# First tiles of a mixture of experts: twelve made of five groups' rows in place of sixteen made of six groups'

## The chip, the cores and the metric

The kernel runs on one core of one Trainium2 chip. The metric is the device time of one execution in microseconds (us), the median over several runs; less is better.

## The reference

The input is 8 sequences of 1024 rows of 128 numbers (float32). Four layers follow each other, each added to its own input after a normalisation of the rows: x = x + layer(layernorm(x)).

1. A delta-rule attention with 4 heads (a short convolution, projections, a triangular solve in each chunk, a state carried from chunk to chunk, a gate, an output projection).
2. A mixture of 8 experts, top 2 of 8 for each row.
3. A linear recurrence along each sequence (three projections, two scans, a ratio, an output projection).
4. The same mixture again, with the same weights.

The mixture is the part that the change touches:

```
logits = xf @ router_w.T                                    # xf: 8192 x 128
topk_probs, topk_idx = top_k(softmax(logits), 2)            # normalised to sum 1
h   = gelu(einsum('nc,ech->neh', xf, w_fc) + b_fc)          # hidden 512
out = einsum('neh,ehc->nec', h, w_proj) + b_proj
y   = einsum('nec,ne->nc', out, combine)                    # combine: two weights a row
```

## The kernel before

The 8192 rows are held in SBUF as 8 groups (g or b, 0 to 7) of 1024 rows, and a group is 8 blocks of 128 rows. The second mixture counts its groups on, 8 to 15. Tiles are counted on in the same way, 0 to 39 and 40 to 79; where a text speaks of tile 12 of a mixture, it is the thirteenth.

**Routing.** For each group, when its rows of the layer before are ready, the kernel normalises them, finds the two experts of each row, and gives every row of every expert a place in a list in HBM (`xs`), where each expert has a region of its own. `place(g)` adds the group's counts to running counts (`run`, two buffers, even and odd groups). POOL then sends the rows: `send(g, n)` issues two indirect DMAs for each block n, so 16 for a group (L633). Their semaphore is `moe_sent0` for even groups and `moe_sent1` for odd ones.

**Tiles.** A tile is 512 rows of one expert's list (full, 31 of them) or 256 (short, 9 of them), 40 in a mixture. The first N_EARLY = 16 tiles are full ones that lie wholly in the rows of the first six groups. Their table (`early_table`: which expert, which row) is made before the last groups are routed. The table of the rest (`route_table`, five pieces) is made when all groups are counted. The constant `short_at` spreads the nine short tiles evenly from position N_EARLY to the last.

**One tile's work.** SP loads the rows (`xt`, L533) and the expert's weights (`wb`, about 1 MB, L498), each into one of four buffers. PE turns the rows (L1761), ACT and DVE split them into a high and a low part (`yTh`, `yTl`), PE multiplies with the first weights (`up`, 12 matmuls, L1773 to L1775), ACT applies the gelu and with DVE splits the result (`hidf`, `hidh`, `hidl`), PE multiplies with the second weights (`down`, 12 matmuls, L1785 to L1787), ACT adds the bias (`out_t`), PE turns the result back (L1795), DVE weighs it (`orow`, L1113), and POOL puts the rows into HBM by one indirect DMA for each block (L671).

**Order.** Each engine runs its own program in order. PE's step t is: turn(t+1), up(t), back(t-2), down(t-1). DVE's step t is: weights(t+1) (the rows' weights, which waits for the rows and the weights of tile t+1), tokens_low(t+1), hidden_low(t) with rows(t-2) in between, and then what is due in this step: choose, weigh and place of the last group in steps 2 and 3, pieces of the table from step TAIL_TABLE on. ACT has tokens_high(t+1) ahead of hidden(t). POOL's step t is: the puts of tile t, and in steps 2 to 5 (TAIL_SEND = 2) two blocks of the last group's sends, that is four DMAs. So the last group of a mixture is routed and sent beside the mixture's first tiles.

**SP's order** around the change (`moe_sync`, L506 to L536): it waits for the early table, loads two tiles' weights, waits for the sends of the first six groups (`sent`, L502), and then goes from tile to tile: rows, then weights. From tile TAIL_FILL = 9 on, in four tiles, it writes two fillers each behind the ends of the experts' lists (L485; the first waits for the counts of all groups). At tile N_EARLY - 2 it waits for the rest's table (L511), at tile N_EARLY for the fillers and for the sends of all groups. Rows and weights of tile t wait until tile t - 4 has left their buffers.

In the first mixture the attention layer's loop runs ahead, in the second the linear recurrence's loop over the groups, where the sends of group b + 5 of the mixture stand in POOL's program a group behind its routing.

Of the kernel before, what the change touches and what calls it, by code (L numbers as in the profile page):

```python
# [18 lines left out]
ALU = mybir.AluOpType  # L19
# [22 lines left out]
def bc(ap, axis, n):  # L42

    v = ap.unsqueeze(axis)
    shape = list(v.shape)
    shape[axis] = n
    return v.to_broadcast(shape)
# [33 lines left out]
def hybrid_kernel(nc, ap, out, phases=4):  # L81
    assert phases == 4
    B, L, _ = ap["hidden"].shape
    NB = B * L // P
    BPB = L // P
    E, _, HID = ap["w_fc"].shape
    HC = HID // P
    GB = 4
    GT = GB * P
# [4 lines left out]
    N_SHORT = N_HALVES - 2 * N_FULL  # L94
    assert N_SHORT >= E
    NT = N_FULL + N_SHORT
    N_EARLY = 16
    N_LATE = N_FULL - N_EARLY
    assert (2 * (B - 2) * L - E * (GT - 1)) // GT >= N_EARLY
    NST = B * L // HT  # L100
    CAP = B * L + HT
    SPARE = E * CAP
# [16 lines left out]
    with ctx:  # L119
        delta_ctx = ExitStack()  # L120

        def sb(name, shape, dt=F32):
            return ctx.enter_context(nc.sbuf_tensor(name, [P] + shape, dt))
# [19 lines left out]
        first = sb("first", [E])  # L143
# [46 lines left out]
        run = sb("run", [2, E, BPB])  # L190
# [72 lines left out]
        base = sb("base", [E])  # L263
        tab1_u = sb("tab1_u", [2, N_EARLY], U32)
        t_e = sb("t_e", [E])
# [55 lines left out]
        def s(name):  # L321
            if name not in SEMS:
                SEMS[name] = sem(name)
            return SEMS[name]
# [68 lines left out]
            return slice(C * k, C * k + C)  # L393

        N_W = 17
        TAIL_ROWS, TAIL_TURN, TAIL_LG, TAIL_RANK, TAIL_SEND, TAIL_TABLE, TAIL_FILL = 0, 1, 2, 3, 2, 5, 9
        W_LIN = 6
        LOADS = ((0, 1), (1, 2), (2, 4), (4, 6), (6, 8))

# [10 lines left out]

        short_at = {N_EARLY + round(j * (NT - 1 - N_EARLY) / (N_SHORT - 1)): j for j in range(N_SHORT)}
        assert len(short_at) == N_SHORT
# [8 lines left out]
        def blocks_of(t):  # L421

            return GB if column[t % NT] < N_FULL else HB
# [14 lines left out]
        def _(sp):  # L438
# [38 lines left out]
            def moe_sync(m):  # L477
                def sm(name):
                    return s(f"moe_{name}")

                def fill_end(e):
                    if e == 0:
                        sp.wait_ge(sm("ends"), m + 1)
                    end = sp.value_load(end_u[0:1, e:e + 1], min_val=0, max_val=SPARE - HT)
                    sp.dma_start(xs[bass.ds(end, HT), :].rearrange("(p j) c -> p j c", j=HB), bc(filler[:, :], 1, HB))\  # L485
                        .then_inc(sm("filled"), 16)

                def entry(row, t):
                    k = column[t - m * NT]
                    return tab1_u[0:1, row, k:k + 1] if k < N_EARLY else tab_u[0:1, row, k:k + 1]  # L490

                def weights(t):
                    b = t % XB
                    e = sp.value_load(entry(1, t), min_val=0, max_val=E - 1)
                    if t >= XB:
                        sp.wait_ge(sm("wts"), t - XB + 1)
                        sp.wait_ge(sm("oT"), t - XB + 1)
                    sp.dma_start(wb[:, b, :].bitcast(F32), wblob[bass.ds(e, 1)].rearrange("a p w -> p (a w)"))\  # L498
                        .then_inc(sm(f"w{b}"), 16)

                def sent(p, groups):
                    sp.wait_ge(sm(f"sent{p}"), 16 * 2 * BPB * groups)  # L502

                t0, ahead = m * NT, 2
                if m == 0:
                    sp.wait_ge(s("p_out"), 16 * N_PREP)  # L506
                    sp.wait_ge(s("p_cst"), 16)
                    sp.wait_ge(s("d_inv"), B)
                else:
                    sp.wait_ge(s("r_took"), B)  # L510
                sp.wait_ge(sm("tab1"), m + 1)  # L511
                for t in range(t0, t0 + ahead):
                    weights(t)
                for p in range(2):
                    sent(p, (m + 1) * B // 2 - 1)
                for t in range(t0, t0 + NT):
                    b, nb = t % XB, blocks_of(t)
                    if 0 <= t - t0 - TAIL_FILL < E // 2:
                        for k in range(2):
                            fill_end(2 * (t - t0 - TAIL_FILL) + k)  # L520
                    if t - t0 == N_EARLY - ahead:
                        sp.wait_ge(sm("tab"), m + 1)
                    if t - t0 == N_EARLY:
                        sp.wait_ge(sm("filled"), 16 * E * (m + 1))
                        for p in range(2):
                            sent(p, (m + 1) * B // 2)
                        if m == 0:
                            sp.wait_ge(s("spare"), 16)
                    row = sp.value_load(entry(0, t), min_val=0, max_val=SPARE)
                    if t >= XB:  # L530
                        sp.wait_ge(sm("T"), t - XB + 1)
                        sp.wait_ge(sm("wts"), t - XB + 1)
                    sp.dma_start(xt[:, b, 0:nb], xs[bass.ds(row, nb * P), :].rearrange("(p j) c -> p j c", j=nb))\  # L533
                        .then_inc(sm(f"x{b}"), 16)
                    if t >= t0 + ahead:
                        weights(t)  # L536
# [171 lines left out]
        def _(ve):  # L708
# [234 lines left out]
            def count_steps(have, base_row, what):  # L943
                ch.link(ve.tensor_tensor(n_e[:, :], have, base_row, ALU.subtract))
                ch.link(ve.tensor_tensor(over[:, :, :], bc(steps[:, :], 1, E), bc(n_e[:, :], 2, NST), what))

            def spans(cols, ks, at_e, end_e):
                n = cols.stop - cols.start
                ve.tensor_tensor(in_e[:, cols, :], bc(tiles[:, ks], 2, E), bc(at_e[:, :], 1, n), ALU.is_ge)
                return ve.tensor_tensor(in_f[:, cols, :], bc(tiles[:, ks], 2, E), bc(end_e[:, :], 1, n), ALU.is_ge)  # L950

            def rows_of_tiles(cols, ks, size, row_e):
                n = cols.stop - cols.start
                return ve.scalar_tensor_tensor(in_f[:, cols, :], bc(tiles[:, ks], 2, E), float(size), bc(row_e[:, :], 1, n),
                                               ALU.mult, ALU.add)
# [12 lines left out]
            short = slice(N_FULL, NT)  # L968

            def early_table(m):  # L970
                count_steps(run[:, 1 - B % 2, :, BPB - 1], first[:, :], ALU.is_le)
                ch.link(ve.tensor_reduce(t_e[:, :], over[:, :, 2:NST].rearrange("p e (k z) -> p e k z", z=2)[:, :, :, 0],
                                         AXX, ALU.add))
                ch.link(ve.tensor_tensor_scan(t_end[:, :], ones_row[:, 0:E], t_e[:, :], 0.0, ALU.mult, ALU.add))
                ve.tensor_scalar(took_to[:, :], t_end[:, :], float(N_EARLY), None, ALU.min)
                ch.link(ve.tensor_tensor(t_at[:, :], t_end[:, :], t_e[:, :], ALU.subtract))
                ch.link(ve.tensor_scalar(took[:, :], t_at[:, :], float(N_EARLY), None, ALU.min))
                ch.link(ve.tensor_tensor(took[:, :], took_to[:, :], took[:, :], ALU.subtract))
                ve.scalar_tensor_tensor(row0[:, :], t_at[:, :], float(-GT), first[:, :], ALU.mult, ALU.add)
                ve.scalar_tensor_tensor(base[:, :], took[:, :], float(GT), first[:, :], ALU.mult, ALU.add)  # L980
                ch.link(spans(early, early, t_at, t_end))
                tile_experts(early, N_EARLY)
                ch.link(rows_of_tiles(early, early, GT, row0))
                tile_rows(early)
                ve.tensor_copy(tab1_u[:, :, :], tab[:, :, early]).then_inc(s("moe_tab1"), 1)
# [87 lines left out]
            def moe_vector(m):  # L1073
# [42 lines left out]
                t0, t1 = m * NT, (m + 1) * NT  # L1116
                weights(t0)
                tokens_low(t0)
                for t in range(t0, t1 + 2):
                    if t + 1 < t1:  # L1120
                        weights(t + 1)
                        tokens_low(t + 1)
                    for c in range(HC):
                        if t < t1:
                            hidden_low(t, c)
                        if c == 1 and t >= t0 + 2:
                            rows(t - 2)
                    if t - t0 == TAIL_LG:
                        choose((m + 1) * B - 1)
                    if t - t0 == TAIL_RANK:  # L1130
                        weigh((m + 1) * B - 1)
                        place((m + 1) * B - 1)
                        route_ends(m)
                    if 0 <= t - t0 - TAIL_TABLE < 5:
                        route_table(m, t - t0 - TAIL_TABLE)

            moe_vector(0)

# [772 lines left out]
```

## Time and profile before

| | us |
|---|---|
| median of 3 runs | 1410.99 (1409.87 to 1417.46) |
| the profiled execution | 1409.89 |
| its span, first to last instruction | 1406.8 |
| busy: PE, DVE, ACT, POOL | 995.6, 1098.6, 717.9, 787.7 |

The first mixture lies at some 592 to 845 us of the span, the second at some 1115 to 1370. Engines: PE = TensorE matmul, PEld = TensorE weight load, DVE = VectorE, ACT = ScalarE, POOL = GpSimd, SP = SyncE, which here only issues DMAs (SPq). L12 is line 12 of the kernel. In a timeline, numbers in square brackets are the idle time of the engine ahead of the instruction and what ended it. Releasers are inferred from semaphore events; "issue" is time in which an engine waits for nothing that the profile shows.

### The profile page before, as it was taken

What the parts mean: (1) busy time and instruction counts of PE and PEld (TensorE: products, weight loads), DVE (VectorE), ACT (ScalarE), POOL (GpSimd) and SP (SyncE); (2) the same over time, 40 slices, a digit from 0 to 9 for tenths busy, and PEclk for the clock granted to TensorE, in tenths of its full rate; (3) what the DMA queues carried; (4) which work ended last, traced back from release to release, by engine and by line L of the source; (5) the groups of instructions that cost most, each with busy time, mean ns of one, the idle gap of its engine ahead of it and who ended that gap; (6) DMA issues with size and microseconds to landing.
All of it is one profiled execution on the core that took longest, in us unless ns stands there. A gap on an engine that the chain in (4) does not pass through costs nothing.

```text
span 1406.8 us, 33043 instructions
## 1 busy us (share of the span) xinstructions
PE 995.6 (71%) x11963; PEld 732.4 (52%) x11963; DVE 1098.6 (78%) x3207; ACT 717.9 (51%) x1534; POOL 787.7 (56%) x670
## 2 busy tenths in 40 slices
PE   4547768668686656399999973665554599999960
PEld 1224455545554445278888861332232478788850
DVE  1188899999999875379888864798988689788845
ACT  2444354452533212077777753765655277777740
POOL 3232256666565552627777661148777747777660
PEclk9768769586785555599999995677676699999985
DMA  5010101111111103138788843012111559788839
GB/s 136 23 45 26 47 26 58 37 47 48 58 59 38 49 28 151 51 133 286 265 280 271 293 138 120 30 49 100 39 38 37 202 181 291 246 292 279 292 103 351
DMA packets 78624, 184.32 MB, mean 131 GB/s; under 512 B 16735, under 2 KB 44826, under 8 KB 68224
## 3 DMA queue, kind: packets, MB, share of 16 engines
q1 hardware_dynamic: 51280, 142.04, 30.3%
q0 software_dynamic: 17280, 35.70, 7.3%
q10 hardware_dynamic: 9904, 4.49, 1.2%
q8 instruction: 96, 1.57, 0.5%
q14 instruction: 64, 0.52, 0.1%
HBM read 131.20 MB, written 52.79 MB: 131 GB/s over the span
## 4 chain that ended last, share of the span: by engine, by line
DVE 28%; PE 27%; POOL 18%; issue 13%; ACT 7%; DMA 6%; SPq 1%; POOLq 0%; DVEq 0%; ACTq 0%
POOL xs L633 7%; POOL res L671 6%; PE ps L1565 5%; DMA res<-orow,idt 3%; POOL rn L616 2%; DVE prod L798 2%; PE ps L1773 2%; PE ps L1774 2%; PE ps L1775 2%; DVE t_p L802 2%; PE ps L1787 2%; PE ps L1785 2%; PE ps L1786 2%; ACT ysc L1247 1%; DVE r_stats L720 1%
## 5 line engine op out<-in xcount | busy, mean ns | idle before, releaser
L671 POOL DMA_INDIRECT res<-orow,idt x284 | 292.1, 1028 | 145.7 <-issue 79.5
L633 POOL DMA_INDIRECT xs<-ysc,slot_u x256 | 283.2, 1106 | 160.2 <-DVE slot_u L941 87.7
L1105 DVE TENSOR_TENSOR hidl<-hidf,hidh 128x512 fp32r<-128x512 f32 (+1 forms) x320 | 198.6, 635 | 21.2 <-ACT hidh L1427 15.4
L1425 ACT ACTIVATE hidf<-ps,wb 128x512 f32<-128x512 f32 (+1 forms) x320 | 198.7, 656 | 4.1 <-PE ps L1775 3.3
L1773 PE MATMUL ps<-yTh,wb 128*128 128x512 f32 (+1 forms) x320 | 126.3, 395 | 0.0
L1785 PE MATMUL ps<-hidh,wb 128*128 128x512 f32 (+1 forms) x320 | 124.6, 389 | 0.0
L1775 PE MATMUL ps<-yTh,wb 128*128 128x512 f32 (+1 forms) x320 | 119.2, 372 | 0.0
L1774 PE MATMUL ps<-yTl,wb 128*128 128x512 f32 (+1 forms) x320 | 119.2, 372 | 0.0
L1787 PE MATMUL ps<-hidh,wb 128*128 128x512 f32 (+1 forms) x320 | 117.9, 368 | 0.0
L1786 PE MATMUL ps<-hidl,wb 128*128 128x512 f32 (+1 forms) x320 | 117.5, 367 | 0.0
L605 POOL TENSOR_TENSOR rstd<-rstd,neg_half 128x8 f32<-128x8 f32 x16 | 27.3, 1709 | 149.4 <-DVE rstd L727 149.3
L1435 ACT ACTIVATE out_t<-ps,wb 128x512 f32<-128x512 f32 (+1 forms) x80 | 51.4, 642 | 113.4 <-PE ps L1787 113.3
L1427 ACT ACTIVATE hidh<-ps,wb 128x512 fp32r<-128x512 f32 (+1 forms) x160 | 103.3, 646 | 0.0
L616 POOL TENSOR_TENSOR rn<-ss,neg_half 128x64 f32<-128x64 f32 x8 | 86.0, 10745 | 30.6 <-DVE ss L751 30.6
L1837 PE MATMUL ps<-lin,w_rkv 128*128 128x512 f32 x96 | 63.0, 813 | 29.3 <-issue 27.9
L1247 ACT ACTIVATE y<-x,shift,rstd 128x128 f32<-128x128 f32 x128 | 51.0, 483 | 60.2 <-POOL shift L606 60.2
L1565 PE MATMUL ps<-yT,tap 128*128 128x512 f32 x128 | 72.5, 718 | 7.0 <-ACT kqm L1305 4.8
L1113 DVE TENSOR_TENSOR orow<-ps,wts 128x512 f32<-128x512 f32 (+1 forms) x80 | 50.0, 624 | 32.7 <-DMA res<-orow,idt 23.8
L623 POOL TENSOR_TENSOR ro<-ro,neg_half 128x16 f32<-128x16 f32 x16 | 50.7, 3168 | 36.8 <-DVE ro L873 36.7
L1828 PE MATMUL ps<-ident,y 128*128 128x128 f32 x64 | 22.7, 432 | 62.7 <-ACT y L1247 57.0
L1775 PEld LDWEIGHTS ps<-yTh,wb 128*128 128x128 f32 x320 | 61.1, 191 | 11.4
L1104 DVE CAST hidh<-hidf 128x512 fp32r<-128x512 f32 (+1 forms) x160 | 66.7, 417 | 0.0
(265 smaller groups left out, 2565.1 us busy)
## 6 DMA issues: line engine op xcount, KB each, us to landing
wb<-wblob SPq DMA_DIRECT2D x80, 1032.0 KB, 5.8
xt<-xs SPq DMA_DIRECT2D x62, 288.0 KB
wblob<-hl SPq DMA_DIRECT2D x16, 512.0 KB
fin<-res SPq DMA_DIRECT2D x14, 512.0 KB, 10.4
hidf<-res SPq DMA_DIRECT2D x10, 512.0 KB, 4.1
res<-orow,idt POOLq DMA_INDIRECT x284
xs<-ysc,slot_u POOLq DMA_INDIRECT x256
rs<-res SPq DMA_DIRECT2D x8, 512.0 KB, 4.4
```

The lines of the kernel that those rows point to most:

```text
L616: pool.tensor_tensor(rn[:, :, :], ss[:, :, :], neg_half[:, 0:2 * HEADS * BPB].rearrange("p (n h) -> p n h", n=BPB), ALU.pow).then_inc(s("d ...
L633: pool.indirect_dma_start(xs[:, :], bass.IndirectOffsetOnAxis(slot_u[:, g % 2, k, n:n + 1], 0), ysc[:, g % 2, n, :], None).then_inc(s(f"mo ...
L671: pool.indirect_dma_start(res[m][:, :], bass.IndirectOffsetOnAxis(idt[:, t % IR, j:j + 1], 0), orow[:, t % OR, j, :], None, bounds_check=2 ...
L1105: ve.tensor_tensor(hidl[:, t % 2, c, 0:n], hidf[:, t % 2, c, 0:n], hidh[:, t % 2, c, 0:n].bitcast(F32), ALU.subtract)\
L1425: ins = act.activation(hidf[:, t % 2, c, 0:n], ps[:, c, 0:n], ACT.Gelu_apprx_tanh, bias=b_col)
L1565: ins = pe.matmul(ps[:, BK_A, :].rearrange("p (j t) -> p j t", j=Q), tap[:, k, :], yT[:, g % 2, r, :, k:k + P], start=k == 0, stop=k == 3)
L1773: pe.matmul(ps[:, c, 0:n], high, yTh[:, t % 2, 0:n], start=True, stop=False)
L1774: pe.matmul(ps[:, c, 0:n], high, yTl[:, t % 2, 0:n], start=False, stop=False)
L1775: pe.matmul(ps[:, c, 0:n], low, yTh[:, t % 2, 0:n], start=False, stop=True).then_inc(sm("fc"), 1)
L1785: pe.matmul(ps[:, 5, 0:n], high, hidh[:, t % 2, c, 0:n], start=(c == 0), stop=False)
L1786: pe.matmul(ps[:, 5, 0:n], high, hidl[:, t % 2, c, 0:n], start=False, stop=False)
L1787: ins = pe.matmul(ps[:, 5, 0:n], low, hidh[:, t % 2, c, 0:n], start=False, stop=(c == HC - 1))
```

## The change

The early tiles are twelve instead of sixteen, made of the rows of the first five groups instead of six. SP's first wait asks for the sends of five groups: three even ones and two odd ones. The early table reads the counts behind the fifth group (the other of the two `run` buffers). The rest's table is made in DVE steps 4, 4, 5, 5 and 6 instead of 5 to 9, the fillers are written from tile 7 on instead of 9, and what is tied to N_EARLY moves with it: SP's wait for the rest's table from tile 14 to 10, its wait for fillers and for the sends of all groups from tile 16 to 12, and the positions of the short tiles from 16 to 39 to 12 to 39. The number of full and short tiles, and the places of the routing and of the sends in the engines' programs, stay.

```diff
--- before.py
+++ after.py
@@ -94,9 +94,10 @@
     N_SHORT = N_HALVES - 2 * N_FULL
     assert N_SHORT >= E
     NT = N_FULL + N_SHORT
-    N_EARLY = 16
+    EARLY_GROUPS = 5
+    N_EARLY = 12
     N_LATE = N_FULL - N_EARLY
-    assert (2 * (B - 2) * L - E * (GT - 1)) // GT >= N_EARLY
+    assert (2 * EARLY_GROUPS * L - E * (GT - 1)) // GT >= N_EARLY and B % 2 == 0
     NST = B * L // HT
     CAP = B * L + HT
     SPARE = E * CAP
@@ -393,7 +394,7 @@
             return slice(C * k, C * k + C)
 
         N_W = 17
-        TAIL_ROWS, TAIL_TURN, TAIL_LG, TAIL_RANK, TAIL_SEND, TAIL_TABLE, TAIL_FILL = 0, 1, 2, 3, 2, 5, 9
+        TAIL_ROWS, TAIL_TURN, TAIL_LG, TAIL_RANK, TAIL_SEND, TAIL_TABLE, TAIL_FILL = 0, 1, 2, 3, 2, (4, 4, 5, 5, 6), 7
         W_LIN = 6
         LOADS = ((0, 1), (1, 2), (2, 4), (4, 6), (6, 8))
 
@@ -512,7 +513,7 @@
                 for t in range(t0, t0 + ahead):
                     weights(t)
                 for p in range(2):
-                    sent(p, (m + 1) * B // 2 - 1)
+                    sent(p, m * B // 2 + (EARLY_GROUPS + 1 - p) // 2)
                 for t in range(t0, t0 + NT):
                     b, nb = t % XB, blocks_of(t)
                     if 0 <= t - t0 - TAIL_FILL < E // 2:
@@ -968,7 +969,7 @@
             short = slice(N_FULL, NT)
 
             def early_table(m):
-                count_steps(run[:, 1 - B % 2, :, BPB - 1], first[:, :], ALU.is_le)
+                count_steps(run[:, (EARLY_GROUPS - 1) % 2, :, BPB - 1], first[:, :], ALU.is_le)
                 ch.link(ve.tensor_reduce(t_e[:, :], over[:, :, 2:NST].rearrange("p e (k z) -> p e k z", z=2)[:, :, :, 0],
                                          AXX, ALU.add))
                 ch.link(ve.tensor_tensor_scan(t_end[:, :], ones_row[:, 0:E], t_e[:, :], 0.0, ALU.mult, ALU.add))
@@ -1131,8 +1132,9 @@
                         weigh((m + 1) * B - 1)
                         place((m + 1) * B - 1)
                         route_ends(m)
-                    if 0 <= t - t0 - TAIL_TABLE < 5:
-                        route_table(m, t - t0 - TAIL_TABLE)
+                    for k in range(5):
+                        if t - t0 == TAIL_TABLE[k]:
+                            route_table(m, k)
 
             moe_vector(0)
```

## Rows read from the trace of the kernel before

**Rows 1.** The page's chain that ended last, shares by engine.

```profile
DVE 28%; PE 27%; POOL 18%; issue 13%; ACT 7%; DMA 6%; SPq 1%; POOLq 0%; DVEq 0%; ACTq 0%
```

**Rows 2.** Window, sum, then busy (x) PE, PEld, DVE, ACT, POOL; clock, DMA.

```profile
665.30:671.75 6.45, 6.45 (x34) 5.29 (x33) 6.17 (x17) 4.72 (x8) 5.03 (x5) 1.00 0.96 322
...
678.20:684.60 6.40, 6.40 (x34) 5.27 (x33) 5.11 (x11) 4.72 (x8) 4.87 (x6) 1.00 0.82 280
```

**Rows 3.** PE's waits, 598 to 845: total us, times, longest.

```profile
PE ps L1795 <- DVE orow L1113: 1.0, 1, 1.0
PE ps L1761 <- DVE yTl L1082: 0.3, 1, 0.3
```

**Rows 4.** PE's waits, 1115 to 1370, the same columns.

```profile
PE ps L1761 <- DMA xt<-xs: 5.7, 1, 5.7
PE ps L1698 <- ACT yTf L1358: 2.7, 1, 2.7
...
PE ps L1795 <- DVE orow L1113: 1.3, 2, 0.9
```

**Rows 5.** SP's own waits, whole run, the same columns.

```profile
SPq L502 <- DMA xs<-ysc,slot_u: 7.8, 1, 7.8
```

**Rows 6.** Chain of waits, second mixture: start us, us, what.

```profile
1107.61 3.87 DMA xs<-ysc,slot_u
...
1112.32 2.98 DMA xt<-xs
...
1115.35 1.13 PE ps L1761 x4
...
1117.12 0.70 DVE yTl L1082
...
1132.09 1.11 PE ps L1698 x4
...
1134.06 0.43 PE ps L1773
...
1135.24 0.23 PE ps L1773
```

**Rows 7.** All engines there in order of time: start us, us, instruction, idle before.

```profile
1102.16 1.51 SPq L498 DMA_DIRECT2D wb<-wblob  x2
...
1109.03 0.64 PE L1716 MATMUL ps<-hit,ones_row 128*128 128x64 f32 x2
...
1111.75 0.17 DVE L941 CAST slot_u<-slot 128x16 uint32<-128x16 f32 x1
...
1121.38 0.39 PE L1773 MATMUL ps<-yTh,wb 128*128 128x512 f32 x1
```

**Rows 8.** Weight loads issued from 1095 to 1125, us to landing.

```profile
DMA to landing us min/median/max: 7.5/7.5/7.5
```

**Rows 9.** SP in order of time, first mixture.

```profile
551.12 2.54 SPq L533 DMA_DIRECT2D xt<-xs  x3
...
663.74 0.35 SPq L533 DMA_DIRECT2D xt<-xs  x1
```

**Rows 10.** PE in order of time, first mixture, turns of tiles 0 and 12.

```profile
591.83 1.06 PE L1761 MATMUL ps<-ident,xt 128*128 128x128 f32 x4
...
671.75 0.60 PE L1761 MATMUL ps<-ident,xt 128*128 128x128 f32 x4
```

**Rows 11.** POOL in order of time, first mixture.

```profile
678.00 0.96 POOL L633 DMA_INDIRECT xs<-ysc,slot_u  x1 [0.30 <-issue]
```

**Rows 12.** POOL in order of time, second mixture.

```profile
1157.61 1.14 POOL L671 DMA_INDIRECT res<-orow,idt  x1 [3.23 <-DVE orow L1113]
...
1201.22 0.96 POOL L633 DMA_INDIRECT xs<-ysc,slot_u  x1 [0.30 <-issue]
```

**Rows 13.** Chain of waits, first mixture.

```profile
683.30 2.77 DMA res<-orow,idt
```

**Rows 14.** PE in order of time, second mixture, turn of tile 12.

```profile
1194.42 0.60 PE L1761 MATMUL ps<-ident,xt 128*128 128x128 f32 x4
```

## The prediction

> **What bounds the kernel now.** I read the chain of waits first. Its shares (DVE 28%, PE 27%, POOL 18%) [rows 1] name no single engine, so each stage has its own limit and the change has to be priced where it acts: at the start of the two mixtures and at the first tile behind the early ones. Inside a mixture I then cut the time into the steps of one tile. A full tile takes 6.4 to 6.5 us, and in such a window PE is busy for the whole of it at full clock, while DVE has 6.17 of 6.45 us, ACT 4.72 and POOL 5.03 [rows 2]. The list of PE's waits agrees: in the first mixture two small waits on DVE of 1.0 and 0.3 us [rows 3], in the second the same kind for 1.3 us and one of 5.7 us for the first rows at its start [rows 4]. So PE sets the end of both mixtures, and a microsecond by which PE stands still is a microsecond of the run, less those few tenths that it now waits for rows. POOL is the engine to watch: from its third tile on it works without a pause, because the last group's sends are queued between its puts.
>
> The change moves two waits of SP. The first stands ahead of the first tile's rows, and only the second mixture pays it now: SP waits once for sends, 7.8 us [rows 5]. The second stands ahead of tile N_EARLY, for ALL sends, those of the last group too. SP now passes it at tile 16, and the trace shows no wait there, the single 7.8 us being all that SP waits for sends in the run [rows 5].
>
> **The change part by part.** *Start of the second mixture.* Now group 13's last send starts at 1107.61 and lands 3.87 us later, the row load leaves at 1112.32 and lands 2.98 us later, and PE turns at 1115.35 [rows 6]. With group 12 as the last one asked for, those sends left before group 13's began, so the 7.8 us wait goes and the load leaves at 1112.32 - 7.8 = 1104.5, right behind the two weight loads that start at 1102.16 [rows 7]. What is late next: those weight loads, which land 7.5 us after issue [rows 8], the second (1.1 us behind the first) at 1110.8. PE is free at 1109.03 + 0.64 = 1109.7, DVE after its slot cast at 1111.75 + 0.17 = 1111.9 [rows 7]. I take rows that land just behind the second weights, at 1111.2: PE turns 4.1 us earlier, and yTl, now at 1117.12 [rows 6], starts 1.77 us after that turn, at 1113.0, when DVE is ready too. Gain 4.1 us; bounds 0 (rows held up by the weights as long as by the wait) and 4.5 (rows there at once, DVE the limit). The Trainium skill (DMA: Bandwidth & Descriptors, section "Two DMAs through the same engine are not ordered") says that descriptors of one queue of an engine start in order; by that the rows queue behind both weight loads and the gain is the 4.1, without it the 4.5. No run here shows rows waited for right behind two weight loads.
>
> The first mixture gains nothing: its early rows leave at 551.12 [rows 9], PE turns them at 591.83 [rows 10], and what PE does until then is the layer before.
>
> *The wait for all sends, now at tile 12.* POOL issues two sends for every 128 rows of the last group behind the puts of mixture steps 2 to 5. Nothing of that moves. POOL starts the last of them at 678.00 in the first mixture [rows 11] and at 1201.22 in the second [rows 12]. But SP issues tile 12's rows at 663.74 [rows 9]. With the wait in front of it, SP stops there for some 17 us. Landing of the last send: 2.77 us is what a put took 5 us later [rows 13], 3.87 us what a send took beside weight loads [rows 6]; I take 2.8, nearest in time. From landing to issue SP takes 1112.32 - (1107.61 + 3.87) = 0.84 us, from issue to PE's turn 1115.35 - 1112.32 = 3.03 us [rows 6]. So tile 12 can be turned 2.8 + 0.84 + 3.03 = 6.7 us after the last send starts: at 678.00 + 6.7 = 684.7. PE now turns it at 671.75 [rows 10]. PE comes to that turn before tile 11's up matmuls and executes in order, so it stands still for 684.7 - 671.75 = 12.9 us. Behind the waiting SP are tile 12's weights and the loads of tiles 13 on; DVE has weights(12) ahead of hidden_low(11), ACT tokens_high(12) ahead of hidden(11). When SP goes on, it issues all of them 1.1 us apart, and up(11) and down(10), whose data are there, keep PE busy for the 6.4 us in which they land. I cost the rest of this burst at nothing; without that cover it would be up to 3 us (a rival).
>
> In the second mixture POOL's unbroken stretch begins with tile 2's puts at 1157.61, which DVE's rows release [rows 12]; these come earlier by the 4.1 us gained, so its last send starts at 1197.1 and the turn can be at 1203.8, against 1194.42 now [rows 14]: 9.4 us later than before, the gain at the start already in it.
>
> *The clock after the stall.* After a wait of 2.7 us [rows 4] PE restarts at 1132.09 with matmuls 0.43 us apart and has them 0.23 apart from 1135.24 [rows 6]: 3.15 us at half speed, 3.15 x (1 - 0.23/0.43) = 1.5 us lost. At the mixture's start the slow stretch ran from 1115.35 to 1121.38 [rows 6, 7], which by the same share is 2.8 us. Bounds 0 and 2.8, taken 1.5, twice.
>
> *What the stall gives back.* PE's waits on late rows and tokens, 1.3 us in each mixture [rows 3, 4], come from POOL's backlog of puts; with PE some 13 us later the backlog is worked off. Minus 1.3, twice.
>
> *Table, fills, order of short tiles.* The table's five pieces go from DVE steps 5 to 9 into 4, 4, 5, 5, 6. DVE has 6.17 us in a step with a piece and 5.11 in one without [rows 2], so the pieces are some 5.3 us; in three steps they make 5.11 + 1.8 = 6.9 us a step, 0.45 over PE's 6.45, some 1.4 us late in all. The fills (eight stores in SP's queue, unchanged in size) leave two tiles earlier, and SP has to wait for the ends table at tile 7; tile 10's rows wait for the table. All of this delays PE ahead of tile 11, where it then waits for tile 12 anyway: hidden by up to 12.9 us, and at most 1.4 us a mixture if that cover were gone. The nine short tiles are spread from 12 instead of 16 on; PE's sum over 40 tiles stays. The smaller early table saves DVE some tenths: nothing.
>
> *Sum.* First mixture 12.9 + 1.5 - 1.3 = +13.1; second 9.4 + 1.5 - 1.3 = +9.6; together +22.7 us. The profiled execution took 1409.89 us (span 1406.8 and 3.1 around it), 1.1 below the median of 1410.99. 1409.89 + 22.7 = 1432.6 us, slower by 1.5%.
>
> **Rivals.** *A: the stall is hidden, only the start's gain is left.* It decides on whether the last send lands before SP needs it, that is by 671.75 - 3.03 - 0.84 = 667.9. For it: rows are loaded up to four tiles ahead, and the chain of waits puts the landing of a put, not PE, on the path in this stretch [rows 13]. Against: the last send starts at 678.00 [rows 11], 10 us too late, and PE has no slack [rows 2]. Time: 1409.89 - 4.1 = 1405.8, faster. Chance 0.07.
>
> *B: the start is not earlier*, because the first rows compete with two weight loads and the sends of group 13 still going out. POOL's tail then stays where it is: second mixture 1201.22 + 6.7 - 1194.42 + 1.5 - 1.3 = 13.7; together 26.8, 1436.7. For it: the weights need 7.5 us there [rows 8]. Against: rows are a quarter of one weight load in bytes. Chance 0.12.
>
> *C: the burst after the stall holds PE a second time*: DVE is stuck on tile 12's weights, and tokens and hidden parts come late by up to 3 us in each mixture: 1432.6 + 6 = 1438.6. Chance 0.10.
>
> *D: part of the stall is given back*, sends issued faster while DVE stands still, no fall of the clock: 1432.6 - 3.0 - some 4 = 1425 to 1426. For it: POOL's backlog is worked off in the stall. Against: POOL's sends have nothing to wait for as it is. Chance 0.10.
>
> **How the numbers follow.** Forecast 0.61, its own range 1429.6 to 1437.4 from the bounds (landing up to 1.1 us later, twice; clock loss 0 to 2.8, twice; the gain at 0 is B). With B, C and D the range is 1422 to 1441; A, and what lies outside the bounds, is left out. Within 0.5% (7 us, about what a measurement can tell from no change) would be up to 1418: 0.04, a stall half hidden. Faster 0.07 is A. Slower 0.89.
>
> **What would show it.** Right: SP waits for sends some 17 us twice, at tile 12 of each mixture; PE has a wait of some 13 us for xt in each, ahead of its twelfth step, with half clock behind it; the first turn of the second mixture is 4 us earlier against the end of group 13's slot cast; POOL's puts and sends look as before. Wrong: PE passes tile 12 without a wait, or the last send is issued before the eighth tile's puts.

## The result, and the profile after

The changed kernel takes 1430.86 us (median of four runs, 1428.07 to 1433.46), the kernel before in the same comparison 1410.65 us (four runs, 1409.87 to 1417.46): a ratio of 1.0142, 95% interval 1.0122 to 1.0163, slower by 20.2 us. The forecast was 1432.6. The profiled execution took 1430.58 us, span 1428.8, against 1409.89 and 1406.8 before.

The page's chain that ended last, shares by engine, of the changed kernel:

```profile
PE 36%; DVE 27%; POOL 14%; issue 10%; ACT 7%; DMA 4%; SPq 1%; POOLq 0%; DVEq 0%; ACTq 0%
```

Against [rows 1], PE has taken 9 points and POOL lost 4. A higher share of PE does not mean more work for PE (998.4 us busy in the whole run against 995.6): less of the chain runs through POOL. What holds PE back is in the waits. SP's own waits after (total us, times, longest):

```profile
SPq L503 <- DMA xs<-ysc,slot_u: 32.8, 2, 16.6
...
SPq L530 <- DVE tab_u L1023: 6.4, 2, 3.3
SPq L485 <- DVE end_u L989: 6.3, 2, 3.2
```

The single wait of 7.8 us for sends [rows 5] has become two, 16.6 and 16.2 us, one at tile 12 of each mixture. The two other lines are new: SP now also waits for the table ahead of tile 10 and for the ends table ahead of the fills. PE's waits after, first in 598 to 860, then in 1095 to 1400 (so that the first of these lines holds the start of the second mixture, 2.5 us, as well as tile 12, 7.7):

```profile
PE ps L1763 <- DMA xt<-xs: 8.2, 1, 8.2
PE ps L1763 <- DVE yTl L1083: 6.4, 4, 3.8
```

```profile
PE ps L1763 <- DMA xt<-xs: 10.1, 2, 7.7
...
PE ps L1763 <- DVE yTl L1083: 3.9, 4, 1.5
```

The waits on `orow` of [rows 3, 4] are gone. The chain of waits at tile 12 of the first mixture (start us, us, what):

```profile
680.10 2.28 DMA xs<-ysc,slot_u
...
683.26 2.29 DMA xt<-xs
...
685.60 0.69 PE ps L1763 x2
686.28 0.43 PE ps L1775
...
690.55 0.43 PE ps L1776
...
691.94 0.23 PE ps L1788
```

It reads downward (`...` marks rows left out): the last send of the last group starts on POOL and lands, SP goes on and issues tile 12's rows, they land, PE turns them and restarts with matmuls 0.43 us apart, later 0.23. SP in order of time shows what stood in its queue:

```profile
665.41 0.33 SPq L499 DMA_DIRECT2D wb<-wblob  x1
683.26 0.33 SPq L534 DMA_DIRECT2D xt<-xs  x1
684.39 0.33 SPq L499 DMA_DIRECT2D wb<-wblob  x1
685.52 0.33 SPq L534 DMA_DIRECT2D xt<-xs  x1
```

Nothing is issued for 17.5 us, then rows and weights go out 1.1 us apart.

To see where the 22 us of the two spans lie, I cut them at PE's turns of the 80 tiles (0 to 39 in the first mixture):

```
                                   before    after     difference
start to turn 0                     591.8    594.4       +2.6
turn 0 to 39, first mixture         231.1    242.5      +11.4
turn 39 to 40, between              292.4    288.7       -3.7
turn 40 to 79, second mixture       229.8    241.8      +12.0
turn 79 to the end                   61.6     61.5       -0.2
```

The first line is not the change: over the ten profiles of this study turn 0 lies between 590.4 and 597.8, with the same instructions ahead of it. The change itself comes to 19.4 us in the profiles, which is close to the 20.2 between the medians.

### The profile page after: what moved, and what is told of

It is laid out like the page before. It is cut to its first block, busy times and chain, and to the rows that moved or that the text cites. A ratio compares the mean times of both kernels' runs of the same rounds, so it can differ in the third digit from the quotient of the medians.

```text
span 1428.8 us, 33040 instructions
## 1 busy us (share of the span) xinstructions
PE 998.4 (70%) x11963; PEld 735.0 (51%) x11963; DVE 1099.8 (77%) x3207; ACT 718.5 (50%) x1534; POOL 786.2 (55%) x670
## 4 chain that ended last, share of the span: by engine, by line
PE 36%; DVE 27%; POOL 14%; issue 10%; ACT 7%; DMA 4%; SPq 1%; POOLq 0%; DVEq 0%; ACTq 0%
POOL xs L634 7%; PE ps L1567 5%; PE ps L1775 3%; PE ps L1777 3%; PE ps L1776 3%; PE ps L1787 3%; PE ps L1789 3%; PE ps L1788 3%; POOL res L672 3%; POOL rn L617 2%; PE ps L1763 2%; DVE prod L799 2%; DVE t_p L803 2%; ACT ysc L1249 2%; PE ps L1797 1%
## 5 line engine op out<-in xcount | busy, mean ns | idle before, releaser
L1106 DVE TENSOR_TENSOR hidl<-hidf,hidh 128x512 fp32r<-128x512 f32 (+1 forms) x320 | 199.6, 635 | 27.0 <-ACT hidh L1429 19.9
L1775 PE MATMUL ps<-yTh,wb 128*128 128x512 f32 (+1 forms) x320 | 128.2, 401 | 0.0
L1777 PE MATMUL ps<-yTh,wb 128*128 128x512 f32 (+1 forms) x320 | 120.6, 377 | 0.0
L606 POOL TENSOR_TENSOR rstd<-rstd,neg_half 128x8 f32<-128x8 f32 x16 | 27.4, 1710 | 148.4 <-DVE rstd L728 148.3
L1777 PEld LDWEIGHTS ps<-yTh,wb 128*128 128x128 f32 x320 | 62.1, 194 | 11.7
L1763 PE MATMUL ps<-ident,xt 128*128 128x128 f32 x284 | 47.2, 286 | 28.8 <-DMA xt<-xs 18.4
L1776 PEld LDWEIGHTS ps<-yTl,wb 128*128 128x128 f32 x320 | 62.6, 196 | 8.8
L1775 PEld LDWEIGHTS ps<-yTh,wb 128*128 128x128 f32 x320 | 62.5, 195 | 8.6
```

Of the source, the lines that this page charges most:

```text
L1106: ve.tensor_tensor(hidl[:, t % 2, c, 0:n], hidf[:, t % 2, c, 0:n], hidh[:, t % 2, c, 0:n].bitcast(F32), ALU.subtract)\
L1775: pe.matmul(ps[:, c, 0:n], high, yTh[:, t % 2, 0:n], start=True, stop=False)
L1776: pe.matmul(ps[:, c, 0:n], high, yTl[:, t % 2, 0:n], start=False, stop=False)
L1777: pe.matmul(ps[:, c, 0:n], low, yTh[:, t % 2, 0:n], start=False, stop=True).then_inc(sm("fc"), 1)
```

## The experiments

The theory: the whole loss is SP's wait for the last send, moved from tile 16 to tile 12, with everything that is in SP's queue and in PE's program behind it. The rivals: the number of groups that the first tiles are made of (five or six) is what costs; the bunched table costs it on DVE; or any other order of the sends would have gained on the kernel before as well. In each run "turn n to m" is read as in the table above, and "step n" of the runs is the time from turn n - 1 to turn n of a mixture, counted from 0; so step 7 ends with the turn of tile 7. Each ratio is against the kernel before as it ran beside that run: 1412.82 us for the first four runs, 1410.53 for the last four.

**Six groups, twelve early tiles.** One part of the change is undone, the other kept.

```diff
-    EARLY_GROUPS = 5
+    EARLY_GROUPS = 6
```

> The changed kernel with six groups again in the first wait and the early table, and twelve early tiles kept. Theory W (the wait for all sends, now at tile 12, makes the loss; the first wait of the second mixture gives a few us back): the start's gain of 3.7 us (the turn of the second mixture's first tile stands 288.7 us behind the first mixture's last turn in the changed trace, 292.4 in the trace of before) is lost, the stalls stay: 1430.9 + 3.7 = 1434.6 us, and SP waits for sends three times, some 8 and twice 16 us. Rival G (reading the counts of five groups, or rows of five groups only, makes the loss): back at 1410.7.

Measured 1432.59 us, ratio 1.0156 (1.0115 to 1.0197). Its SP waits:

```profile
SPq L503 <- DMA xs<-ysc,slot_u: 40.6, 3, 17.3
```

The two long waits stay and the one at the start of the second mixture is back. The mixtures take 243.8 and 242.5 us, as after; the stretch between them takes 291.5 us instead of 288.7. That stretch also holds the linear recurrence, so I count from group 13's slot cast too (the cast of the places its sends go to): the second mixture's first turn comes 29.9 to 30.7 us behind it in the four runs with six groups, and 26.5 to 27.4 in those with five groups and the weights ahead of the rows. So the groups decide the start, worth some 3 us, and not the stall. The run's time alone could not show it: its interval holds that of the changed kernel.

**Six groups, fourteen early tiles.** The wait for all sends is put two tiles later; the bunched table stays.

```diff
-    EARLY_GROUPS = 5
-    N_EARLY = 12
+    EARLY_GROUPS = 6
+    N_EARLY = 14
```

> Six groups and fourteen early tiles; the table in DVE steps 4, 4, 5, 5, 6 and the fillers from tile 7 as in the changed kernel. Theory W: PE would turn tile 14 at 684.6 us of the trace of before, the last send allows it at 684.7 less the 1.2 us by which the changed trace was quicker, so there is no stall: 1410.7 to 1413 us. Rival T (the bunched table on DVE, the earlier fillers and the short tiles' new places make the loss, not the sends): most of it stays, 1425 us or more.

Measured 1413.31 us, ratio 1.0011 (0.9991 to 1.0031): the loss is gone with the table still bunched. SP waits 18.5 us in three pieces, and PE has no wait for rows behind tile 0, because those rows are asked for early enough. What the table costs shows in the chain of waits of this run, in its step 7:

```profile
637.25 0.69 DVE hidl L1106
637.95 0.09 DVE n_e L945
...
638.52 0.42 DVE t_e L996
...
640.30 0.09 DVE halves L1007
640.42 0.24 DVE wsel L1094
```

From 637.95 to 640.39 DVE works at the table while the rows of a tile wait for it. Turns 4 to 12 take 54.9 and 55.1 us where the kernel before takes 52.0 and 52.3, with steps 7 and 8 at 7.3 and 8.0 in the first mixture instead of 6.4. Much of it is won back by turn 39: the mixtures take 231.7 and 231.2, only 0.6 and 1.4 over the kernel before.

**Sends one step earlier.**

```diff
-        TAIL_ROWS, TAIL_TURN, TAIL_LG, TAIL_RANK, TAIL_SEND, TAIL_TABLE, TAIL_FILL = 0, 1, 2, 3, 2, (4, 4, 5, 5, 6), 7
+        TAIL_ROWS, TAIL_TURN, TAIL_LG, TAIL_RANK, TAIL_SEND, TAIL_TABLE, TAIL_FILL = 0, 1, 2, 3, 1, (4, 4, 5, 5, 6), 7
```

> The changed kernel with the last group's sends in POOL's steps 1 to 4 instead of 2 to 5: one tile's puts (5.1 us) and POOL's idle 3.4 us ahead of tile 2's puts fall out of the time ahead of the last send. Theory W: both stalls are shorter by some 8.5 us: 1430.9 - 17 = 1414 us. Rival T: nothing of table, fillers or short tiles is changed, 1431 us.

Measured 1415.29 us, ratio 1.0035 (1.0013 to 1.0057). The last send of the first mixture:

```profile
669.09 0.95 POOL L634 DMA_INDIRECT xs<-ysc,slot_u  x1 [0.30 <-issue]
```

That is 78.7 us behind this run's first turn (590.39), where the changed kernel has 85.7: 7.0 us sooner, and some 9 in the second mixture; 8.5 were expected. SP still waits for sends, but PE's only wait for rows is 2.3 us, at the start of the second mixture:

```profile
SPq L503 <- DMA xs<-ysc,slot_u: 14.8, 2, 7.7
```

```profile
PE ps L1763 <- DMA xt<-xs: 2.3, 1, 2.3
```

SP's wait has only halved, yet PE's stall is gone and with it three quarters of the loss. A wait of SP costs only the part by which the rows come after PE is there. Of the quarter that is left, 3.2 and 2.4 us lie in the mixtures (234.3 and 232.2 us), where turns 4 to 12, with the table still bunched, take 56.1 and 56.5. The stretch between the mixtures takes 291.0 us, but the 2.4 us more than after lie ahead of group 13's cast; from there to the turn it is 26.5, so the start's gain is kept.

**All sends in two steps.** Sends from step 1 on, four blocks of 128 rows per step instead of two.

```diff
-        TAIL_ROWS, TAIL_TURN, TAIL_LG, TAIL_RANK, TAIL_SEND, TAIL_TABLE, TAIL_FILL = 0, 1, 2, 3, 2, (4, 4, 5, 5, 6), 7
+        TAIL_ROWS, TAIL_TURN, TAIL_LG, TAIL_RANK, TAIL_SEND, TAIL_TABLE, TAIL_FILL = 0, 1, 2, 3, 1, (4, 4, 5, 5, 6), 7
...
-                    if 0 <= k < BPB // 2:
-                        for n in range(2):
-                            send((m + 1) * B - 1, 2 * k + n)
+                    if 0 <= k < BPB // 4:
+                        for n in range(4):
+                            send((m + 1) * B - 1, 4 * k + n)
```

> The changed kernel with the last group's sends in POOL's steps 1 and 2, four blocks (eight sends) in each, so that the last send stands ahead of tile 3's puts. POOL would start it some 20 us earlier than now, at some 656 of the first mixture's time in the trace of before, and it lands before SP wants tile 12's rows at 663.7. Theory W: no stall, the start's gain is left: 1410.65 - 3.7 = 1407 us, plus up to 3 us if tile 7's weighing on DVE has to wait for tile 3's puts. Rival T: 1431 us.

Measured 1409.88 us, ratio 0.9987 (0.9969 to 1.0005). The last send of the first mixture:

```profile
658.83 0.96 POOL L634 DMA_INDIRECT xs<-ysc,slot_u  x1 [0.30 <-issue]
```

That is 65.8 us behind the first turn (593.00), 19.9 sooner than in the changed kernel, and SP's wait for sends is 0.2 us in the whole run:

```profile
SPq L503 <- DMA xs<-ysc,slot_u: 0.2, 1, 0.2
```

This is the strongest evidence for the theory: with the sends out in time, twelve early tiles of five groups cost nothing that the time shows. The stretch between the mixtures keeps its gain (288.9 us). What is left over is mainly the table: turns 4 to 12 take 55.9 and 55.8, and PE in order of time has these waits in steps 7 to 9 of the first mixture (in brackets the idle time and its releaser):

```profile
641.69 0.63 PE L1763 MATMUL ps<-ident,xt 128*128 128x128 f32 x4 [1.13 <-DVE yTl L1083]
649.85 0.63 PE L1763 MATMUL ps<-ident,xt 128*128 128x128 f32 x4 [1.50 <-DVE yTl L1083]
657.24 0.63 PE L1763 MATMUL ps<-ident,xt 128*128 128x128 f32 x4 [0.77 <-DVE yTl L1083]
```

**The same sends in the kernel before.** The edit of the last run alone, on sixteen tiles of six groups.

> The kernel before (six groups, sixteen early tiles) with the last group's sends in POOL's steps 1 and 2, four blocks in each, as in the fourth run. Theory W: SP does not wait at tile 16 and the start's wait stays, so the sends' place is worth nothing there: as the kernel before, some 1411 to 1413 us. Rival S (the earlier sends themselves save time, by themselves): 3 us or more below it.

Measured 1413.57 us, ratio 1.0018 (1.0001 to 1.0035). No gain by itself: the mixtures take 231.5 and 229.8 us against 231.1 and 229.8. Early on the eight sends in a row even cost something: DVE waits 3.4 and 3.8 us for a put queued behind them to land, and turns 0 to 12 take 83.1 and 81.4 us instead of 79.9 and 79.1, which is won back by turn 39. So the order of the sends gives back the loss of the change and is no improvement that would hide it.

**The table spread out.** On top of the sends in two steps:

```diff
-        TAIL_ROWS, TAIL_TURN, TAIL_LG, TAIL_RANK, TAIL_SEND, TAIL_TABLE, TAIL_FILL = 0, 1, 2, 3, 1, (4, 4, 5, 5, 6), 7
+        TAIL_ROWS, TAIL_TURN, TAIL_LG, TAIL_RANK, TAIL_SEND, TAIL_TABLE, TAIL_FILL = 0, 1, 2, 3, 1, (4, 5, 6, 7, 8), 8
...
-                    if t - t0 == N_EARLY - ahead:
+                    if t - t0 == N_EARLY:
                         sp.wait_ge(sm("tab"), m + 1)
```

> The fourth run's kernel (five groups, twelve early tiles, sends in POOL's steps 1 and 2) with the table's pieces in DVE steps 4 to 8, the fillers from tile 8, and SP's wait for the table at tile 12 instead of 10. PE's turns of tiles 4 to 12 took 55.9 and 55.8 us in the fourth run against 52.0 and 52.3 before, with steps 7 and 8 the long ones. If the bunched table does that (theory W's account), these 8 turns are back at some 52 us and each mixture is shorter by what it did not win back later, 0.3 to 1.7 us: 2 us under the fourth run, some 1406 to 1408. If POOL's puts, which stand behind the eight sends, do it, steps 7 to 9 stay long: no change.

Measured 1409.50 us, ratio 0.9990 (0.9975 to 1.0005). Steps 7 and 8 are back at 6.4 to 6.5 us in both mixtures. The edit also moves the fillers and SP's wait for the table, but PE's waits in these steps were for DVE, so the bunch on DVE is the likely cause. But turns 4 to 12 take 53.7 and 53.6, not the 52 of the kernel before: step 9 of the first mixture now takes 8.1, with a wait of PE for rows of 1.6, and steps 10 and 11 of the second 7.0 and 7.5. The trace shows what stands there. In the first mixture the load of these rows is issued at 649.39; of the sixteen updates by which its semaphore tells of the landing, fourteen are there by 652.76 and the last comes at 658.19; what held it is not shown. In the second, DVE has a piece of the table ahead of each late yTl, for which PE waits 0.4 and 0.9 us. The 2 us that were expected do not show: the ratio hardly differs from 0.9987, that of the sends in two steps with the table bunched. One crowding of the first dozen steps has been exchanged for a smaller one.

**Ten early tiles.** On the changed kernel, to test the size of the stall from the other side.

```diff
-    N_EARLY = 12
+    N_EARLY = 10
```

> The changed kernel with ten early tiles, so that SP waits for all sends at tile 10. Theory W: the end of the sends stays and PE stands before tile 10 instead of 12, two steps of 6.45 us longer, in both mixtures: 1430.9 + 25.8 = 1456.7 us. Rival T (table, fillers, short tiles): within 3 us of the changed kernel.

Measured 1456.62 us, ratio 1.0329 (1.0311 to 1.0347). The mixtures take 255.5 and 253.6 us, 13.0 and 11.8 over the changed kernel's; two steps of 6.45 are 12.9. SP's waits, and PE's in the first mixture:

```profile
SPq L530 <- DVE tab_u L1023: 29.9, 2, 15.0
SPq L503 <- DMA xs<-ysc,slot_u: 29.7, 2, 14.9
```

```profile
PE ps L1763 <- DMA xt<-xs: 19.8, 2, 10.8
```

PE now stands twice in each mixture, at tile 8 for the table (10.8 us) and at tile 10 for the sends (9.0 us), and yet the loss is only that of the tiles that no longer lie ahead of the last send. The last send is the fixed point (86.4 and 84.8 us behind the mixture's first turn), and each tile that moves behind it costs a step. Turn 10 comes 91.8 and 90.3 us behind the first turn, as turn 12 does after the change (91.2 and 91.3): what PE stands for the table it no longer stands for the sends.

**The first rows ahead of the weights.** On top of the spread table, the first tile's rows are issued before the first two weight loads.

```diff
-                for t in range(t0, t0 + ahead):
-                    weights(t)
...
+                    if t == t0:
+                        for k in range(t0, t0 + ahead):
+                            weights(k)
```

> The sixth run's kernel with the first tile's rows issued ahead of the first two weight loads of a mixture. In the changed trace yTl of the second mixture's first tile starts 2.15 us behind group 14's slot cast (5.37 before). If the rows are late because they stand behind two weight loads, they land some 5 us earlier, DVE is the limit, and yTl starts some 0.9 us behind the cast: 1.2 us less than the sixth run. If the first weights' landing is the limit, no change or up to 1 us more, as the weights now go 1.1 us later.

Measured 1407.59 us, ratio 0.9982 (0.9971 to 0.9993): below both kernels, by 0.18% against the one before; its interval overlaps that of the spread table (0.9975 to 1.0005), so against that run the gain is read from the trace. SP in order of time at the start of the second mixture:

```profile
1102.55 0.35 SPq L532 DMA_DIRECT2D xt<-xs  x1
1103.71 1.47 SPq L499 DMA_DIRECT2D wb<-wblob  x2
1106.09 1.45 SPq L532 DMA_DIRECT2D xt<-xs  x2
```

Then DVE's slot cast of group 14 and the first tile's yTl:

```profile
1112.34 0.17 DVE L943 CAST slot_u<-slot 128x16 uint32<-128x16 f32 x1
...
1113.04 0.69 DVE L1084 TENSOR_TENSOR yTl<-ps,yTh 128x512 fp32r<-128x512 f32 x1
```

yTl starts 0.70 us behind the cast, against 2.15 after the change and 5.37 in the kernel before. The stretch between the mixtures takes 286.0 us instead of the spread table's 289.0, but the second mixture 232.2 instead of 230.6, and half of the gain is lost again: the second tile's rows now come behind the weights, and PE waits 3.6 us for them:

```profile
PE ps L1764 <- DMA xt<-xs: 3.6, 1, 3.6
```

This is PE's only wait for rows in the stretch from 1095 to 1400.

## Why the prediction was right

*The stall, and where it is anchored.* The step held in its form and nearly in its size. PE's turns of tiles 0 and 12 after, first mixture, then tile 12 of the second:

```profile
594.39 1.06 PE L1763 MATMUL ps<-ident,xt 128*128 128x128 f32 x4
...
685.60 0.69 PE L1763 MATMUL ps<-ident,xt 128*128 128x128 f32 x2 [8.21 <-DMA xt<-xs]
...
1216.85 0.69 PE L1763 MATMUL ps<-ident,xt 128*128 128x128 f32 x2 [7.68 <-DMA xt<-xs]
```

POOL in order of time shows the last send of each mixture:

```profile
680.10 0.96 POOL L634 DMA_INDIRECT xs<-ysc,slot_u  x1 [0.30 <-issue]
...
1211.40 0.96 POOL L634 DMA_INDIRECT xs<-ysc,slot_u  x1 [0.30 <-issue]
```

Counted from the mixture's first turn that is 85.7 and 85.8 us, against 86.2 and 85.9 before [rows 6, 10 to 12]: POOL's tail keeps its distance from the start of the mixture to within half a microsecond, as predicted. From the last send to PE's turn it took 2.28 + 0.88 + 2.34 = 5.5 us instead of 6.7. The estimate took the landing from a put and the load from a full tile; tile 12 is now a short tile with half the bytes. In both mixtures this is 1.2 us too much. Turn 12 stands 11.3 us later against turn 0 in the first mixture (forecast 12.9) and 12.2 in the second (13.5, which is the forecast's 9.4 net and the 4.1 of the start).

*PE's wait was not the 13 us that I named as its sign.* It is 8.2 and 7.7 us, and the stall is no smaller for that: PE came to the turn late as well, delayed mainly by the table on DVE: turn 11 lies 2.9 us later against turn 0 than before in the first mixture, and 4.4 in the second, where the first steps were slower too. This cover was costed at 1.4 us, from 0.45 us a step; it measured 3.0 (54.9 against 52.0 for turns 4 to 12, with six groups and fourteen early tiles). The stall hides it, as the prediction said. It had added up DVE's work over three steps; two pieces in one step also stand ahead of the next tile's rows in DVE's order, and PE waits for these rows (its waits for yTl in the run with the sends in two steps).

*The clock.* Windows of the changed kernel around the two restarts, then the rest of the first mixture from tile 13's turn (window, sum, busy (x) of PE, PEld, DVE, ACT, POOL; granted clock, DMA share, GB/s):

```profile
685.60:691.10 5.50, 5.50 (x14) 4.34 (x15) 0.87 (x5) 3.59 (x6) 4.28 (x5) 0.51 0.92 345
...
1216.85:1224.60 7.75, 7.75 (x31) 6.28 (x32) 3.25 (x9) 4.06 (x7) 5.92 (x7) 0.79 0.96 359
```

```profile
694.34:836.85 142.51, 142.51 (x805) 121.94 (x804) 118.54 (x285) 109.11 (x208) 94.12 (x92) 1.00 0.81 273
```

After 8.2 us of standing still PE ran for 5.5 us at a granted clock of 0.51, the lower level of 1.2 GHz, and then at 1.00. From tile 12's turn to tile 13's it took 8.7 us instead of 6.4, a loss of 2.3; in the second mixture, after 7.7 us, it had 0.50 for only 3.05 us (1216.85 to 1219.90), took 7.8 and lost 1.3. The forecast was 1.5 for each, with bounds of 0 and 2.8.

*What the stall gives back.* The same stretch of the kernel before, tile 13's turn to tile 39's:

```profile
678.17:822.92 144.75, 143.24 (x804) 121.21 (x802) 120.17 (x288) 109.33 (x208) 105.27 (x103) 1.00 0.81 275
```

PE was idle for 1.5 us in it and is idle for none after; the stretch is 2.2 us shorter, and 1.6 in the second mixture. The forecast was 1.3 in each, from PE's waits alone. POOL has less to do in the window, 94.1 us instead of 105.3: its backlog of puts was worked off while PE stood. But the stall is not needed for it: with six groups and fourteen early tiles, where PE never stood there, the same stretch takes 142.3 us and POOL has 102.0, so the 3 us by which the table had held PE up were enough.

*The start of the second mixture.* SP, then DVE and PE there, after the change:

```profile
1115.42 1.51 SPq L499 DMA_DIRECT2D wb<-wblob  x2
1117.80 2.58 SPq L534 DMA_DIRECT2D xt<-xs  x3
```

```profile
1125.19 0.17 DVE L942 CAST slot_u<-slot 128x16 uint32<-128x16 f32 x1
1125.57 0.71 PEld L1763 LDWEIGHTS ps<-ident,xt 128*128 128x128 f32 x4 [2.65 <-DMA xt<-xs]
...
1127.34 0.69 DVE L1083 TENSOR_TENSOR yTl<-ps,yTh 128x512 fp32r<-128x512 f32 x1 [1.05 <-ACT yTh L1417]
```

The rows leave right behind the two weight loads, and PE turns them 0.38 us after group 14's slot cast instead of 3.60 [rows 6, 7]: 3.2 us gained, 3.3 against group 13's cast, 3.7 in the stretch between the mixtures. The forecast was 4.1. Its price of 7.5 us for the weights ahead of the rows was read from another load: of the four loads in the window of [rows 8] the view tells the landing of one, that issued at 1115.97, behind the rows. So it does after, where the one is issued at 1121.22:

```profile
DMA to landing us min/median/max: 8.3/8.3/8.3
```

For the two loads ahead of the rows the semaphore updates in the traces have 5.2 and 7.6 us from issue to the last update before, 5.1 and 8.05 after. So 7.5 came close to the second of them by luck. After the change that load is down at 1124.63 and the rows at 1125.52, just behind it, as the forecast had it; the load took half a microsecond longer than forecast, and the rows came 0.9 us behind it instead of 0.4. From the rows' issue to the turn it took 7.8 us, where the same load with no weights just ahead took 3.03 [rows 6]; with the rows issued first, DVE's yTl came 1.4 us sooner behind the cast. The Trainium skill (DMA: Bandwidth & Descriptors, section "Two DMAs through the same engine are not ordered") says that descriptors in one queue of an engine start in order. The landings agree: weights, weights, rows at 1120.51, 1124.63 and 1125.52 after, and rows, weights, weights at 1105.51, 1110.93 and 1114.01 with the rows issued first.

*The rest of the second mixture.* The first four steps took 1.4 us more there, at a granted clock of 0.76 in the fourth (0.89 before), which the forecast did not have. It cost nothing, since turn 12 waits for POOL in any case.

*The sum, in one table* (us; from PE's turns):

```
                                        forecast   measured
turns 0 to 12, first mixture             +12.9      +11.3
turn 12 to 13, clock                      +1.5       +2.3
turn 13 to 39, given back                 -1.3       -2.2
between the mixtures                      -4.1       -3.7
turns 0 to 12, second mixture            +13.5      +12.2
turn 12 to 13, clock                      +1.5       +1.3
turn 13 to 39, given back                 -1.3       -1.6
tail                                       0         -0.2
sum                                      +22.7      +19.4
```

The mechanism is the one that was forecast, but that the time lies in the range is in part luck. The larger errors lie on one side: both stalls were taken too large (1.6 and 1.3 us) and what is given back too small (0.9 and 0.3). The range had no bound for a landing sooner than taken, which is what happened (1.2 us, twice). Its lower end, 1429.6, came from a clock that costs nothing, and the clock cost 2.3 and 1.3. The 19.4 us of the profiles, put on the 1409.89 that the forecast started from, would be 1429.3, just below the range; the profiled 1430.58 also holds the 2.6 us ahead of turn 0 that are not the change's.

*The rivals.* A (the stall hidden) is false for this kernel, but it is what the sends in two steps make true: 1409.88. B (no gain at the start) is false: 3.2 to 3.7 of 4.1 came. C (the burst holds PE a second time) did not show: PE is busy throughout from tile 12's turn to tile 13's in both mixtures, and from there to turn 39 of the first. D (part given back) came true in a small part, 0.9 and 0.3 us more than forecast, by puts worked off; its other half, sends issued faster and no fall of the clock, did not: the last four sends start 1.26 to 1.53 us apart (1.26 to 1.78 before), and the clock fell.

Open is why the clock's return took 2.3 us from the first mixture and 1.3 from the second after waits of nearly the same length, and why the spread table still leaves 1.3 to 1.7 us in steps 9 to 11: why one row load lands so late in the first mixture, and why the table's last pieces hold PE up in the second, which they did not in the kernel before.

## What to carry to other kernels

Price a wait in an in-order queue from the event it waits for, not from its length: find when the last producer is done, add landing, issue and load, and compare with when the consumer gets there; here SP's waits of 16 us cost 11 to 12 each, and those of 7 to 8 (sends one step earlier) did not hold PE up. Then look for what is queued behind it on every engine that runs in program order: here PE stood in front of one turn, and the matmuls behind it ran without a wait once it was done. When such a wait has to move forward, move its producer first: here the same change was free once the last send left some 20 us sooner.

## What was not expected of the hardware

The same row load took 7.8 us from issue to use behind two weight loads and 3.03 us without them, although it is little more than a quarter of one weight load in bytes (288 of 1032 KB); here the order of issue mattered more than the size. And little of the crowding on DVE or POOL in the first dozen steps reaches the end. With the table bunched, turns 4 to 12 took 3.0 and 2.8 us more than before (six groups, fourteen early tiles), and the whole mixtures 0.6 and 1.4 more. With eight sends in a row on POOL in the kernel before, turns 0 to 12 took 3.2 and 2.4 us more, and the whole mixtures 0.4 and nothing.
